# A four-layer network on one core: linear ramps for the column weights, a new order at the deformable stage's entry, and two normalisations done half by half

## What is computed

```
L0: 7x7 local attention;         top-2 of 8 experts
L1: 3x3 L1-distance convolution; expert choice (16 experts, 8 tokens each)
L2: two deformable 3x3 samplings with batch norm, 1x1 conv; top-2 of 8 experts
L3: full 256x256 attention, 4 heads, relative positions; expert choice
```

## Time and profile before

| | |
|---|---|
| three runs | 414.03, 414.09, 414.76 us; median 414.09 |
| the profiled execution | 414.42 us, span of its instructions 412.6 us |
| busy | PE 378.3 (92%), DVE 332.2 (81%), ACT 289.0 (70%), POOL 166.4 (40%) |
| granted TensorE clock, mean | 0.996 of full speed |
| L1's distances | 51 to 119 us |
| deformable turn 0, turn 1 | 143 to 231, 231 to 318 us |
| L2's experts, normalisation 6 | 324 to 338, 338 to 343 us |
| attention of L3 | 343 to 388 us |

### The profile page before, as it was taken

One profiled execution on the slowest core, in us unless ns is written; L12 is line 12 of the kernel. 1 busy time (PEld: TensorE's weight loads), 2 busy tenths in 40 slices (PEclk: granted clock), 3 DMA queues, 4 the chain that ended last, 5 costly groups with the idle time before them and its releaser, 6 DMA issues.

```text
span 412.6 us, 9850 instructions
## 1 busy us (share of the span) xinstructions
PE 378.3 (92%) x3996; PEld 259.4 (63%) x3996; DVE 332.2 (81%) x658; ACT 289.0 (70%) x514; POOL 166.4 (40%) x142
## 2 busy tenths in 40 slices
PE   6889999899899998899999998999999999999897
PEld 6676932223247756666677665667678786666575
DVE  3799697998973487999999587999996786999451
ACT  3865396998936579997760599977822627999471
POOL 5004100000000069899997378999994050001000
PEclk9999999999999999999999999999999899999999
DMA  7300040000015000000000000000000000000000
GB/s 302 140 3 0 2 98 2 2 0 2 2 37 243 2 2 2 2 2 3 2 2 0 2 2 2 2 2 2 2 2 1 2 2 1 2 2 1 2 2 27
DMA packets 1629, 9.29 MB, mean 23 GB/s; under 512 B 208, under 2 KB 976, under 8 KB 1104
## 3 DMA queue, kind: packets, MB, share of 16 engines
q1 hardware_dynamic: 1440, 8.59, 5.8%
q10 hardware_dynamic: 144, 0.07, 0.1%
HBM read 7.40 MB, written 0.26 MB: 19 GB/s over the span
## 4 chain that ended last, share of the span: by engine, by line
DVE 35%; PE 30%; ACT 14%; POOL 11%; issue 8%; DMA 1%; DVEq 0%; SPq 0%; ACTq 0%
PE bank L1434 6%; PE bank L1153 4%; POOL PRD L377 4%; DVE wb L1010 3%; PE bank L1514 3%; DVE PRD L1010 3%; ACT RINGS L679 3%; ACT RINGS L609 2%; DVE RINGS L908 2%; ACT RINGS L612 2%; DVE RINGS L899 2%; POOL RINGS L407 2%; POOL wb L377 2%; PE bank L1423 2%; PE bank L1497 2%
## 5 line engine op out<-in xcount | busy, mean ns | idle before, releaser
L1514 PE MATMUL bank<-VB,RINGS 64*128 64x144 f32 x1152 | 93.1, 298 | 6.2 <-DVE PRD L1010 3.1
L1514 PEld LDWEIGHTS bank<-VB,RINGS 64*128 64x128 f32 x1152 | 75.6, 186 | 28.1 <-issue 9.8
L1153 PE MATMUL bank<-cst 128*128 128x128 f32 x424 | 61.7, 289 | 0.0
L1153 PEld LDWEIGHTS bank<-cst 128*128 128x128 f32 x424 | 55.2, 200 | 5.5 <-issue 3.0
L360 POOL TENSOR_TENSOR HY<-OM,cst 128x324 f32<-128x324 f32 x16 | 11.6, 749 | 116.5 <-DVE LXA L955 112.6
L1010 DVE TENSOR_TENSOR wb<-bank,HY 128x864 f32<-128x864 f32 x48 | 50.4, 1050 | 5.0 <-PE bank L1514 4.8
L609 ACT ACTIVATE RINGS<-bank,cst 128x768 f32<-128x768 f32 x48 | 42.4, 884 | 15.2 <-PE bank L1497 15.1
L1010 DVE TENSOR_TENSOR PRD<-bank,HY 128x864 f32<-128x864 f32 x48 | 50.1, 1050 | 3.7 <-PE bank L1514 3.7
L612 ACT ACTIVATE RINGS<-RINGS,cst 128x768 f32<-128x768 f32 x48 | 45.0, 937 | 1.6
L550 ACT ACTIVATE RINGS<-PRD,wb 128x2048 f32<-128x2048 f32 (+1 forms) x21 | 39.4, 1918 | 4.5 <-PE bank L1434 3.5
L1434 PE MATMUL bank<-RINGS,cst 128*32 128x512 f32 x336 | 39.7, 594 | 2.4 <-DVE RINGS L908 2.0
(11 more groups left out here) (280 smaller groups left out, 692.6 us busy)
## 6 DMA issues: line engine op xcount, KB each, us to landing
wd<-in_wd SPq DMA_DIRECT2D x1, 2793.0 KB, 9.5
wb<-in_wb SPq DMA_DIRECT2D x1, 2112.0 KB, 9.8
wc<-in_wc SPq DMA_DIRECT2D x1, 1027.0 KB, 11.8
cst<-in_cst SPq DMA_DIRECT2D x1, 766.0 KB, 5.1
PRD<-PRD SPq DMA_DIRECT2D x1, 324.0 KB, 3.6
PRD<-PRD SPq DMA_DIRECT2D x1, 323.9 KB, 4.7
PRD<-PRD SPq DMA_DIRECT2D x1, 323.8 KB, 4.7
XC<-in_x SPq DMA_DIRECT2D x2, 128.0 KB, 2.4
```

The source lines that it names most:

```text
L1153: pe.matmul(bk[:, 0:P], ident, ident, start=True, stop=True)
L1514: ins = pe.matmul(view(bank[q % 2 * 2 + gp], k3 * NR, [[3 * NR, 2 * CG], [1, NR]]), view(HX, b % 2 * HXN + (3 * t + k3) * NPIX + half * P, ...
```

## The change

1. **Ramps.** The hat becomes the second difference of a ramp: `hats` makes only max(0, 16 - column + ...) in one Relu pass from PSUM, and the values are taken from second differences of the image instead. So ACT writes the image into a zero-padded XP, and POOL takes two differences (`second_differences`) in the place of ACT's copy to XW. LXT gets its own Relu at the image's left edge (same instruction count), the mask is multiplied by a clipped edge weight (`right_edge` on ACT, `modulation` on DVE), the value bias by an edge factor BV. `spread` now waits for `hat_ready` of the hats before, as there is no `abs_done`.
2. **Entry.** Four groups of points (POINTS) go one way: `om` lands on a base in banks 4, 0/1, 3 and 7 and DVE reads it there (`offsets` and the second kind of `points` go). Row distances of images 2 and 3 move from POOL (`rows_off`) to ACT (`rows_apart` with count 2, placed by PAIR_ROWS_AFTER: nine passes of 144 elements). `based` lays one 432-column base more, a second is laid inside the turn. The order on PE and DVE is new.
3. **Normalisations 2 and 6** are done half by half, each half to its end; DVE and ACT take half 1 after half 0. In 6 the first half is turned, copied and projected alone; scores of group 0 start on it, half 1 is projected inside group 0. POOL makes heads 1 to 7 and adds `bu1` to XT. The head copies are of one half. `keep_warm` of 12 products in each goes down to 1 and 3, and to 1 and 2.

The diff, cut to its core:

```diff
-NORM_BANKS = ((0, 7), (0, 3), (0, 1), (0, 5), (5, 3), (0, 5), (0, 1), (0, 5))
+NORM_BANKS = ((0, 7), (0, 3), (0, 1), (0, 5), (5, 6), (0, 5), (0, 6), (0, 5))
+FILL_KEYS, FILL_FIRST, FILL_QUERIES = 3, 1, 2
-FILL_HOP, FILL_PROB, FILL_DRAIN = 2, 8, 3
+FILL_HOP, FILL_PROB, FILL_DRAIN = 2, 4, 3
+FILL_SPREAD, FILL_APART = 6, (1, 3)
+PAIR_ROWS_AFTER = {(0, 1): (0, 2), (0, 2): (2, 5), (1, 0): (5, 7), (1, 1): (7, 9)}
+ROWS_AFTER = {(1, 2): (0, 2), (2, 0): (2, 3), (2, 1): (3, 4), (2, 2): (4, 5), (3, 0): (5, 6), (3, 1): (6, 7), (3, 2): (7, 9)}
+        POINTS = ((0, 1, 0, 2, bank[4], 3 * KG), (1, B4 - 1, 0, 2, bank[0], 512), (B4, B4, 0, 1, bank[3], 0), (B4, B4, 1, 1, bank[7], 0))
 POOL
+            def second_differences(turn, bh):
+                pool.wait_ge(xp_ready, n)
+                pool.tensor_tensor(view(XD, xd, [[XPW - 1, HH], [1, XPW - 1]]), shifted(1), shifted(0), ALU.subtract).then_inc(xd_ready, 1)
+                pool.tensor_tensor(view(XW, bh * NR * NA * WW, [[NA * WW, NR], [WW, NA], [1, WW]]), shifted(1), shifted(0),
+                                   ALU.subtract).then_inc(xw_ready, 1)
             for turn in range(2):
+                second_differences(turn, 0)
                 rows_off(turn, 0)
                 rows_off(turn, 1)
                 masked(turn, 0)
-                rows_off(turn, 2)
-                rows_off(turn, 3)
+                second_differences(turn, 1)
+            for gr in range(1, GROUPS3):
+                pool.wait_ge(qs_ready, bh + 1)
+                pool.tensor_tensor(QC[:, h * F + bh * NPIX:h * F + (bh + 1) * NPIX], view(QS, bh * NPIX, [[1, NPIX]]),
+                                   view(cst, CST["hm"] + h, [[0, NPIX]]), ALU.mult).then_inc(heads_ready, 1)
 ACT
+            def deviations_apart(n, eps, between=None):
+                for bh in range(NBH):
...
+                    if bh == 0 and between is not None:
+                        between()
             def hats(i, t):
-                act.activation(view(HX, hx, [[NPIX, 3], [1, NPIX]]), view(bank[4], 0, [[512, 3], [1, NPIX]]), ACT.Abs,
-                               bias=cv("mx", 1)).then_inc(abs_done, 1)
-                act.wait_ge(abs_done, 3 * i + t + 1)
-                act.activation(view(HX, hx, [[1, 3 * NPIX]]), view(HX, hx, [[1, 3 * NPIX]]), ACT.Relu, scale=-1.0,
-                               bias=cv("one", 1)).then_inc(hat_ready, 1)
+                act.activation(view(HX, hx, [[NPIX, 3], [1, NPIX]]), view(bank[4], 0, [[512, 3], [1, NPIX]]), ACT.Relu, scale=-1.0,
+                               bias=cv("mx", 1)).then_inc(hat_ready, 1)
-            norm(6, "eps6", then=ACT.Exp)
-            for h in range(3):
-                heads(h)
+            deviations_apart(6, "eps6", first_half)
+            act.activation(QC[:, 0:NPIX], bank[4][:, 0:NPIX], ACT.Identity, scale=cv("hm", 1, 0), bias=bqh[:, 0:1]).then_inc(qc_ready, 1)
+            act.activation(view(QS, 0, [[1, NPIX]]), bank[4][:, 0:NPIX], ACT.Identity, bias=...).then_inc(qs_ready, 1)
+            table(ACT.Exp)
 DVE
             def deform(turn):
-                first_points(turn, bank[4], 3 * KG, 0, 1)
-                first_points(turn, bank[0], 512, 1, B4 - 1)
-                values(turn)
-                offsets(turn, 0)
-                offsets(turn, 1)
-                points(B4, B4)
+                points(turn, 0)
+                points(turn, 1)
+                modulation(turn, 0)
+                values(turn)
+                modulation(turn, 1)
+                points(turn, 2)
+                points(turn, 3)
+                modulation(turn, 2)
                 for b in range(B):
                         sample(i, *divmod(u, 2))
+                        if b == 0 and u == 0:
+                            modulation(turn, 3)
+            norm(6, mixed_done, 3, meanwhile=lambda: keys3(0))
+            values_by_head(0)
+                if gr == 0:
+                    dve.wait_ge(xn_turned, turned(6, 1))
+                    dve.tensor_copy(XNC[:, NPIX:F], bank[NORM_BANKS[6][1]][:, 0:NPIX]).then_inc(xnc_ready, 1)
                 weights(4 * gr)
+                if gr == 0:
+                    second_half()
 PE
-                after(pe, abs_done, 3 * i + t)
+                after(pe, hat_ready, 3 * i + t)
-                values(0, bank[2], 0, 4)
+                based_late(bank[7], 1)
                 turn_points(turn, 0)
-                values(0, bank[2], 4, NR).then_inc(val_done, 1)
+                values(0, bank[2], 0, NR).then_inc(val_done, 1)
+                offsets(bank[3], 0, B4, B4, 0)
                 spread(turn, 0)
-                for half in range(2):
-                    offsets(bank[half], 0, B4, B4, half)
-                keep_warm(bank[7], FILL_HATS)
-                spread(turn, 1)
-                spread_at = {1: 2, 3: 3, 5: 4, 6: 5}
+                offsets(bank[7], 0, B4, B4, 1)
+                spread_at = {0: 1, 1: 2, 3: 3, 5: 4, 6: 5}
+            keep_warm(bank[0], FILL_FIRST)
+            turn_half(0)
+            keep_warm(bank[5], FILL_QUERIES)
+            project3(0, bank[1][:, 0:NPIX], bank[4][:, 0:NPIX], bank[5][:, 0:NPIX])
             scores3(0)
-            keep_warm(bank[4], FILL_PROB)
+            pe.wait_ge(xt_kept, 6)
+            turn_half(1)
+            keep_warm(bank[7], FILL_PROB)
             for gr in range(GROUPS3):
                 turn3(4 * gr)
                 if gr == 0:
-                    keep_warm(bank[6], FILL_DRAIN)
+                    project3(1, bank[6][:, 0:NPIX], bank[6][:, NPIX:F], bank[7][:, NPIX:F])
```

More of the change, by code:

```diff
@@ L355, in rows_off @@
             def rows_off(turn, b):
[L357 removed]
+                pool.wait_ge(lxa_ready, pointed(turn, b))
                 after(pool, prod_used, IMQ * B * turn)
@@ L694, in _ @@
                     probabilities(4 * gr + i)
-                    if gr == 0 and i == 0:
-                        heads(3)
                     if gr and i == 0:
@@ L727, in per_tile, with norm @@
                 return view(t, 0, [[1, NT], [0, C]])
-            def norm(n, sums=None, first=0, step=1):
+            def norm(n, sums=None, first=0, step=1, meanwhile=None):
                 half = NT // 2
@@ L735, in norm @@
                 one = lambda t, bh: t[:, bh * half:(bh + 1) * half]
+                if n in APART:
+                    for bh in range(NBH):
+                        dve.wait_ge(sums, first + step * bh)
+                        link(dve.tensor_reduce(one(s16, bh), x(bh), AX.X, ALU.add))
+                        dve.scalar_tensor_tensor(of(XN, bh), per_tile(s16, bh), -1.0 / C, x(bh), ALU.mult, ALU.add).then_inc(centred, 1)
+                        dve.wait_ge(sq_made, NBH * n + bh + 1)
+                        dve.tensor_reduce(one(var, bh), of(SQ, bh), AX.X, ALU.add).then_inc(var_ready, 1)
+                        if bh and meanwhile is not None:
+                            meanwhile()
+                        dve.wait_ge(sd_ready, NBH * n + bh + 1)
+                        link(dve.reciprocal(one(rstd, bh), one(sd, bh)))
+                        dve.tensor_tensor(of(XN, bh), of(XN, bh), per_tile(rstd, bh), ALU.mult).then_inc(xn_ready, 1)
+                    dve.wait_ge(xn_ready, NBH * (n + 1))
+                    return
                 for bh in range(NBH):
@@ new lines, in modulation @@
+            def modulation(turn, group):
+                b, count, first, halves, bk, half_step = POINTS[group]
+                dve.wait_ge(edge_ready, grouped(turn, group))
+                for half in range(halves):
+                    at = (2 * b + first + half) * KG
+                    ins = dve.scalar_tensor_tensor(view(MM, at, [[2 * KG, count], [1, KG]]), view(LX, at, [[2 * KG, count], [1, KG]]), 1.0,
+                                                   view(bk, half * half_step + 2 * KG, [[3 * KG, count], [1, KG]]), ALU.min, ALU.mult)
+                ins.then_inc(mm_ready, 1)
@@ L1474, in based, with based_late @@
                               skip_group_check=True)
+                based_late(bank[3], 0)
+            def based_late(bk, half):
+                pe.matmul(bk[:, 0:12 * KG], ident, view(base, half * 3 * KG, [[0, 4], [1, 3 * KG]]), start=True, stop=False,
+                          skip_group_check=True)
             based()
@@ L1486, in turn_points @@
                     pe.wait_ge(val_used, VALUE_PIECES * turn + b - 2)
+                if b == 1:
+                    pe.wait_ge(mm_ready, grouped(turn, 3))
                 for half in range(2):
-                    ins = pe.transpose(bank[7][0:LXW, half * P:(half + 1) * P], view(LXA, (b * 2 + half) * LXW, [[1, LXW]]), ident)
+                    ins = pe.transpose(bank[7 if b else 6][0:LXW, half * P:(half + 1) * P], view(LXA, (b * 2 + half) * LXW, [[1, LXW]]), ident)
                 ins.then_inc(t_done, 1)
@@ L1566, in deform @@
                     if n in values_at:
-                        piece = values_at[n]
+                        piece, first, end = values_at[n]
```

(4 more changed lines are left out.)

276 lines of the change are left out of this document (172 added, 104 removed).

## The result

The changed kernel takes **410.04 us** (median of 4 runs, 409.76 to 410.85), the kernel before 414.06 in the same comparison: ratio 0.9898, 95% interval 0.9887 to 0.991, which is 3.7 to 4.7 us less. The forecast was 409.0 with a range of 406.2 to 412.2. The profiled execution took 410.12 us, its span 408.3.

A forecast was written before the change was run, and what follows sets the result against it. ACT bounds each turn's first images, DVE and POOL the later ones, DVE and ACT the attention; elsewhere hand-overs count. Gains 0.9 + 1.7 + 2.5 = 5.1 from 414.42 give 409.3, for the median 409.0 us; range 406.2 to 412.2.

The forecast's parts named there:

- Normalisation 2: Behind L0's experts: done half by half, L1's first tap comes at 50.95 instead of 51.88; gain 0.9 us.
- The deformable turns: Both turns: one hat pass less nets 1.3 us each, less 0.85 between them; gain 1.7 us.
- Sample 0 starts within 0.2 of before: Entry of a turn: DVE's four groups cost about what `offsets` and `points` did, so the first sample hardly moves.
- Image 0 loses 0.8: First image of a turn: image 1's first sample comes at 161.3 instead of 160.53.
- Images 1, 2 and 3: Early images of a turn: they take 9.0, 8.9 and 8.8 us, gaining 1.5 + 0.2 + 0.4.
- The 144-element passes: Nine passes added on ACT in images 0 and 1, 0.36 us each; five, 1.8 together, counted before image 1's first hat.
- The base between the turns: Bank 3's base in the chain ahead of the `om` product: turn 1 starts 0.7 to 0.85 us later.
- rival (d): Deformable turns: 48 spreads each wait for a whole hat, 0.2 us a step, 9.6 lost; 418.6 us, chance 0.07.
- rival (b): Deformable turns: nine new ACT passes cost 0.61 us each, the stage loses 1.2; 411.9 us, chance 0.18.
- The attention: L2's experts to the attention: first scores 3.95 us earlier, part given back, group 1 gains 2.5.
- (a): Deformable turns: ACT's relief passes on, images 1 to 3 go at DVE's pace, 4.9 us gained; 405.8 us, chance 0.14.
- (c): Thinned normalisation 6: TensorE's clock falls, keys, queries and scores take double, +2.2 us; 411.2 us, chance 0.11.

The follow-up runs named there:

- e7: The changed kernel without the two covering products on PE between product 0 and product 1 of each turn: 409.56 us.
- e6: The changed kernel with row distances of images 2 and 3 back on POOL, instead of nine 144-element passes on ACT: 410.06 us.
- e5: The changed kernel with turn 1's base of bank 3 laid in turn 0's tail, in place of the six covering products there: 409.47 us.
- e9: The changed kernel with a second ACT pass for each hat, spreads released by the first pass and products by the second: 416.77 us.
- e12: The kernel before with only the change's three additional columns of constants, unused: 414.24 us.
- e8: The changed kernel with DVE's copy of half 1 in normalisation 6 after the second tile of scores instead of the fourth: 409.57 us.
- e10: The changed kernel without covering products in normalisations 2 and 6 and behind the first scores: 411.21 us.
- e1: The changed kernel with normalisation 2 done whole again, 12 covering products ahead of its products: 411.28 us.
- e4: The changed kernel with turn 1's base of bank 3 laid behind the covering products in turn 0's tail, which stay: 410.49 us.
- e2: The changed kernel with everything from normalisation 6 to the attention as before the change: 412.26 us.
- e11: The changed kernel with e5, e6, e7 and e8 together, and one covering product instead of six in turn 1's tail: 408.15 us.
- e3: The kernel before with only the deformable turns changed, normalisation 2 and all from normalisation 6 on as before: 413.51 us.

## Why the forecast was right, and where not

**The total** was right (409.0 against 410.04, within the range), partly by luck: the medians show 0.4 more than the trace from the copy on, a start that no step had. Since the copy the sum is 3.6 where 5.1 was forecast.

**Normalisation 2**: +0.68 for +0.9. Right in every hand-over but the last: half 0 was ready and half 1 begun where the step put them (its sum at 44.82, in the old count 45.56 for 45.5), the last first-tap pass at 51.2 instead of 50.95. PE's spread of half 1 began 0.2 late. Mis-sized, mechanism right.

**The deformable turns**: +0.95 for +1.7. The net of a turn, 1.02 in turn 0 for 1.3, looks right, and its step was wrong on both sides. "Sample 0 starts within 0.2 of before" failed: it came 0.79 earlier in both turns. The paragraph before it had the first hat end 0.6 earlier and did not carry that on. "Image 0 loses 0.8" failed as well: from sample 0 to image 1 it took 9.24 instead of 7.83, 1.4 more, of which e7 puts 0.37 on two covering products that the step costed at nothing; they had lain beside other work and were moved onto the path. From the offsets product to image 1 the loss is 0.62, for 0.8. Images 1, 2 and 3 took 9.07, 9.13 and 8.95 for 9.0, 8.9 and 8.8. The 144-element passes took 0.34 each of ACT for 0.36, but mostly in its waits: e6 finds 0.2 a turn where the step laid five of them, 1.8, on the path. The base between the turns cost 0.72, inside 0.7 to 0.85, and e5 shows that it need not have. The end of turn 1 lost 0.28, in no step. All of it lies ahead of the first sample of the last image, which starts 1.23 after the sample before it, where it took 0.96 before the change. First the changed kernel, then e9:

```profile
298.42 1.05 DVE L1091 TENSOR_TENSOR PRD<-bank,HY 128x864 f32<-128x864 f32 x1
299.65 1.06 DVE L1091 TENSOR_TENSOR wb<-bank,HY 128x864 f32<-128x864 f32 x1 [0.18 <-issue]
```

```profile
306.88 1.06 DVE L1093 TENSOR_TENSOR wb<-bank,HY 128x864 f32<-128x864 f32 x1 [0.18 <-issue]
```

"Issue" says that the profile shows nothing that DVE waited for. It is not rival (d): e9's spreads are released by the first of two passes again, and it has the same wait and the same 0.28. All twelve kernels with the new deformable stage have it at this one sample of turn 1, and none in turn 0, where PE does the same beside it; the kernel before and e12 have it nowhere. What holds DVE there is open.

Some of the working is loose, without weight for the total: 1.3 + 1.3 - 0.85 is 1.75, "3.0 twice less 1.0" is 5.0, and rival (b)'s loss of 1.2 doesn't follow from its own net of a turn (nothing gained gives 0.85, 0.3 lost a turn gives 1.45).

**The attention**: +1.99 for +2.5. Counted from the end of L2's experts, which lie 2.32 earlier than before, the first minimum came at 343.93 for 343.5: from the end of half 0's copy to ACT's head it took 1.36 and the head itself 0.56, where 1.1 and 0.4 had been counted. Of the lead of 3.52 gained there 1.53 was given back, for 1.45. The step named the right reason, half 1's projection behind DVE's copy, and took it as given; e8 moves the copy and has 0.95 back.

**The rivals.** (a) fell: ACT is not full, and images 1 to 3 still take 0.6 to 0.8 more than DVE's 8.34 (0.4 of it in images 2 and 3 is the values). ACT's relief does pass on, 3.3 a turn by e9, but to pay for image 0. (b) fell, 0.34 a pass. (c) did not happen in the changed kernel; it did happen in the traced execution without the covers (e10); the Trainium skill's rule in "TensorE: Matmul & The Clock Gate", section "What's actually happening", that the throttled clock is the default and activity releases it, agrees with e10's trace. (d) fell: in the late images of turn 0 every sample keeps its distance from the first of image 4 within 0.01 of before.

## What to carry to other kernels

A net of a few tenths can be the difference of large terms: here a pass worth 6.6 us paid for an order that cost 5.7, and only putting the pass back showed it. A covering product is free only while the next real product has to wait for something else anyway, so look at each of them for that; where they are thinned, look at the granted clock of several executions, not of one. And count milestones from the first event behind the start before two traces are compared.

## What the runs showed of the hardware

The granted clock fell to its 1.2 GHz level in 12 of the 14 profiled executions while PE had work, for some microseconds each time and at places that change: at 31 to 35 us in the changed kernel, e1, e4, e7 and e12; at 322 to 340 in before, e2, e5, e6, e9 and again e12; at 313 to 316 and 323 to 326 in e11; at 339 to 343 and 346 to 350 in e10; nowhere in e3 and e8. In the 7 us before each of these falls PE was busy for 5.97 to 6.96 us, only in e10 for 4.80 and 5.07. In the changed kernel it was 5.98, and while the clock was low PE was busy throughout:

```profile
30.00:36.00 6.00, 6.00 (x50) 4.75 (x49) 5.45 (x18) 3.88 (x8) 0.63 (x2) 0.72 0.00 0
```

What makes it fall there is open, but these falls go with an early start (e12). What one costs depends on where it lands: nothing measurable at 31 to 35 us, where e1 and e12 keep step with the trace of before, which has none there; nothing at 326 to 330 in the trace of before, since e3 without a fall gains nothing on it there; 0.36 at 322 to 329 in e5, 0.54 in L2's experts in e2, 2.65 for the two in the attention's beginning in e10.

And an ACT pass with a strided output of 144 elements, 0.54 us long, lets the next begin after 0.34 us, one of 288 after 0.62 (medians; 0.61 in the earlier trace rows): 0.28 for 144 elements more. A whole contiguous pass of 768, 0.90 long, lets the next begin after 0.80.
